# A whole-round order list, and only inverse roots left on GpSimd, in a four-layer graph network kernel

## The reference

```
attn = softmax(masked scores); o = attn @ v
x2 = layernorm(x1 + o @ Wo + bo) * g2 + be2
y  = layernorm(x2 + gelu(x2 @ W1 + b1) @ W2 + b2) * g3 + be3
x  = layernorm(x + y)
```

## Time and profile before

| | |
|---|---|
| median of three runs | 2414.89 us |
| the profiled execution | 2414.36 us |
| its span, first to last instruction | 2412.5 us |
| TensorE busy | 2108.8 us, 87% |
| VectorE busy | 1676.3 us, 69% |
| ScalarE busy | 1367.9 us, 57% |
| GpSimd busy | 380.9 us, 16% |
| mean granted TensorE clock | 0.948 of full |

### The profile page before, as it was taken

One profiled execution on the slowest core, in us unless ns is written; L12 is line 12 of the kernel. 1 busy time (PEld: TensorE's weight loads), 2 busy tenths in 40 slices (PEclk: granted clock), 3 DMA queues, 4 the chain that ended last, 5 costly groups with the idle time before them and its releaser, 6 DMA issues.

```text
span 2412.5 us, 56320 instructions
## 1 busy us (share of the span) xinstructions
PE 2108.8 (87%) x21445; PEld 1816.0 (75%) x21445; DVE 1676.3 (69%) x4767; ACT 1367.9 (57%) x3387; POOL 380.9 (16%) x400
## 2 busy tenths in 40 slices
PE   8979569898888989898989888898989898989886
PEld 5634458888787868787888778786878788888875
DVE  6779456767676766776676767676677667676844
ACT  4557335555555646565556555565656565555554
POOL 0000111112121212121121112121212112111200
PEclk9989789999999999999999999999999999999997
DMA  7867100000000000000000000000000000000000
GB/s 265 277 238 268 53 10 2 2 28 2 29 2 27 2 28 2 28 2 29 2 2 28 2 29 2 27 2 29 2 28 2 29 2 2 28 2 10 2 10 10
DMA packets 37903, 92.68 MB, mean 38 GB/s; under 512 B 2544, under 2 KB 27120, under 8 KB 33392
## 3 DMA queue, kind: packets, MB, share of 16 engines
q1 hardware_dynamic: 37616, 88.86, 10.7%
HBM read 55.29 MB, written 33.55 MB: 37 GB/s over the span
## 4 chain that ended last, share of the span: by engine, by line
PE 57%; DVE 13%; issue 12%; ACT 5%; POOL 2%; DMA 0%; DVEq 0%; POOLq 0%; ACTq 0%
PE ps L260 16%; PE ps L262 15%; PE ps L261 15%; PE ps L1063 4%; POOL rstd L1476 2%; DVE stats L1549 2%; PE ps L1132 1%; PE ps L1274 1%; DVE pool_mem L1686 1%; DVE x L1580 1%; PE ps L1045 1%; DVE pool_mem L1670 1%; DVE pool_mem L1689 1%; PE ps L1054 1%; ACT hl_b L1328 1%
## 5 line engine op out<-in xcount | busy, mean ns | idle before, releaser
L1384 ACT ACTIVATE pool_mem<-ps,lstm_b 128x128 f32<-128x128 f32 (+2 forms) x1248 | 440.1, 411 | 329.6 <-PE ps L262 322.6
L260 PE MATMUL ps<-hl_a,w_hi 128*128 128x256 f16 (+2 forms) x1984 | 478.9, 264 | 59.4 <-DVE hl_a L1697 21.6
L261 PE MATMUL ps<-hl_a,w_hi 128*128 128x256 f16 (+2 forms) x1984 | 477.5, 264 | 0.0
L262 PE MATMUL ps<-hl_a,w_lo 128*128 128x256 f16 (+2 forms) x1984 | 477.2, 263 | 0.0
L1476 POOL TENSOR_TENSOR rstd<-ve,nhalf 128x2 f32<-128x2 f32 x224 | 182.7, 816 | 1404.9 <-DVE ve L1556 1404.9
L260 PE MATMUL ps<-hl_b,w_hi 128*128 128x168 f16 (+2 forms) x1408 | 354.6, 261 | 5.3 <-DVE hl_b L1697 3.8
L261 PE MATMUL ps<-hl_b,w_hi 128*128 128x168 f16 (+2 forms) x1408 | 354.6, 260 | 0.0
L262 PE MATMUL ps<-hl_b,w_lo 128*128 128x168 f16 (+2 forms) x1408 | 354.5, 260 | 0.0
L260 PE MATMUL ps<-pool_mem,w_hi 128*128 128x128 f16 (+2 forms) x1536 | 329.8, 241 | 21.3 <-DVE pool_mem L1691 21.2
L261 PE MATMUL ps<-pool_mem,w_hi 128*128 128x128 f16 (+2 forms) x1536 | 329.5, 241 | 0.0
L262 PE MATMUL ps<-pool_mem,w_lo 128*128 128x128 f16 (+2 forms) x1536 | 329.2, 240 | 0.0
(11 more groups left out here) (234 smaller groups left out, 4859.1 us busy)
## 6 DMA issues: line engine op xcount, KB each, us to landing
xa<-in_x SPq DMA_DIRECT2D x32, 512.0 KB, 5.5
h_scratch<-pool_mem SPq DMA_DIRECT2D x16, 1024.0 KB, 4.3
pool_mem<-h_scratch SPq DMA_DIRECT2D x16, 1024.0 KB, 7.1
pool_mem<-in_wpack SPq DMA_DIRECT2D x16, 704.0 KB, 4.0
o_scratch<-act_in SPq DMA_DIRECT2D x16, 512.0 KB, 2.9
act_in<-o_scratch SPq DMA_DIRECT2D x16, 512.0 KB, 4.8
out<-xb SPq DMA_DIRECT2D x16, 512.0 KB, 3.4
row<-in_rows SPq DMA_DIRECT2D x1, 1408.0 KB, 10.8
```

Of the source, the lines that this page charges most:

```text
L260: nc.tensor.matmul(o, l[0], r[0], start=first, stop=False, skip_group_check=True)
L261: nc.tensor.matmul(o, l[0], r[1], start=False, stop=False, skip_group_check=True)
L262: return nc.tensor.matmul(o, l[1], r[0], start=False, stop=last, skip_group_check=True)
L1384: op = nc.scalar.activation(gates[s][:, g, m * w:(m + 1) * w], ps[s][:, g, m * w:(m + 1) * w], ACT.Tanh, bias=lstm_b[:, bias:bias + 1], sc ...
```

## The change

1. `x1_bias` and `x2_bias` are gone. The products of `attn_out` and `mlp_down` get one more matrix multiplication for each 128 nodes: a matrix of ones times a matrix whose rows 0 and 32 hold the high and low part of the bias (the rest is zero).
2. The multiplication of the probabilities moves from GpSimd's `probs` into VectorE's `invert_sums`.
3. `xa_bias` moves to VectorE as `shift_xa`, works in place on xa, and stands early in the tile, soon after `norm_g1`. With it xa is read until `norm_g3`, so the transfer of the next x waits for that step.
4. GpSimd keeps the roots.
5. ORDER and the rule that plays it twice give way to ROUND, a list of a whole round, in which each entry names its stream (0 or 1) and, by `:` or `+`, whether it belongs to this tile of the stream or to its next one. The two halves of the list need not be alike.
6. SyncE's loop asks for both streams' next inputs before it stores both; the signal gat_ok starts one tile ahead, so that `turn_y` can wait for the previous tile's last step.

```diff
+ROUND = """
+1:norm_g1.1 1:xa_bias.1 1:k.0 0:inp4 0:cell4 1:scores.0 1:turn_x1.1 1:exps.0 0:hid4 0:inp5 1:v.1 1:q.1 1:turn_probs.0
+1:k.1 0:cell5 0:hid5 1:attend.0 1:scores.1 1:exps.1 0:inp6 1:attn_out.0 1:norm_g2.0 1:turn_probs.1 0:cell6 0:hid6
...
+0:turn_xc.1 0:gat_mix.0 1:gcn1.1 0:gat.1 0:norm_l3.0 0+turn_y.0 1:inp0 1:cell0 0+norm_l0.0 1:hid0 1:inp1 0:gat_exps.1
...
+def rounds(n):
+    return [(name, s, n + after if after else n) for s, after, name in ROUND]
...
+                for j, name in enumerate(("bo", "b2")):
+                    nc.vector.tensor_scalar(abias[0:1, j, :], row[0:1, ROWS.index(name), :], WSCALE, None, ALU.mult)
...
                 def load_next(s, n):
...
-                        sp.wait_ge(*pre_ok.at(s, n, h, "xa"))
+                        sp.wait_ge(*ln_step.at(s, n, h, "l1.t"))
...
-                        if with_sums:
-                            mm = nc.tensor.matmul(tok(s, bank)[:, b, :], sums[:, 0:P], gbias[:, 0, :], start=False, stop=True,
+                        if with_row is not None:
+                            mm = nc.tensor.matmul(tok(s, bank)[:, b, :], with_row[0], with_row[1], start=False, stop=True,
...
-                    dense(s, h, hl_a[s], h * HTOK, "wo", BANK_B[h]).then_inc(tok_ps.of(s, h), 1)
+                    dense(s, h, hl_a[s], h * HTOK, "wo", BANK_B[h], (ones_row[:, :], abias[:, 0, :])).then_inc(tok_ps.of(s, h), 1)
...
-                def probs(s, n, h):
...
                 def invert_sums(s, n, h):
...
+                        dve.wait_ge(*smax_ok.at(s, n, h, f"inverse{b}"))
+                        nc.vector.tensor_tensor(prob[s][h][:, b, :, :], prob[s][h][:, b, :, :],
+                                                ssum[s][:, i:i + HEADS].unsqueeze(2).broadcast_to([P, HEADS, P]), ALU.mult)\
+                            .then_inc(prob_ok.of(s, h), 1)
...
                 def add_attn(s, n, h):
-                    dve.wait_ge(*pre_ok.at(s, n, h, "x1"))
...
-                                                                     xb[s][:, blocks(h), :], ALU.mult, ALU.add))
+                                                                     x1[s][:, blocks(h), :], ALU.mult, ALU.add))
...
+                def shift_xa(s, n, h):
+                    dve.wait_ge(*feat_ps.at(s, n, h, "xp"))
+                    dve.wait_ge(*x_ok.at(s, n, h, "x1"))
+                    nc.vector.tensor_tensor(xa[s][:, blocks(h), :], xa[s][:, blocks(h), :], half_row("be3"), ALU.add)\
+                        .then_inc(pre_ok.of(s, h), 1)
```

More of the change, by code:

```diff
@@ L77 @@
 PARTS = 2
[L78 to L83, removed]
@@ L84 @@
-mix1.0 gcn0.1 gcn1.0 mix1.1 gcn1.1 inp0 cell0
-""".split()
[L86 to L102, removed]
+ROUND = """
@@ new lines @@
+1:norm_g1.1 1:xa_bias.1 1:k.0 0:inp4 0:cell4 1:scores.0 1:turn_x1.1 1:exps.0 0:hid4 0:inp5 1:v.1 1:q.1 1:turn_probs.0
+1:k.1 0:cell5 0:hid5 1:attend.0 1:scores.1 1:exps.1 0:inp6 1:attn_out.0 1:norm_g2.0 1:turn_probs.1 0:cell6 0:hid6
+1:turn_x2.0 1:attend.1 0:pack4 1:attn_out.1 1:norm_g2.1 1:mlp_up.0 1:gelu_split.0 0:inp7 1:turn_x2.1 0:cell7
+1:mlp_down.0 0:hid7 1:mlp_up.1 1:norm_g3.0 1:gelu_split.1 0:inp8 0:cell8 0:hid8 1:mlp_down.1 1:norm_g3.1 0:inp9
+0:cell9 0:hid9 1:norm_l1.0 1:norm_l1.1 0:inp10 0+norm_y 0:cell10 0:hid10 1:mix0.0 1:mix0.1 0:turn_state.0 0:norm_l2.0
@@ new lines @@
+0:turn_state.1 1:gcn0.1 1:gcn0.0 0:turn_xc.0 1:mix1.1 1:mix1.0 0:gat.0 0:gat_exps.0 0:norm_l2.1 1:gcn1.0 0:turn_att.0
+0:turn_xc.1 0:gat_mix.0 1:gcn1.1 0:gat.1 0:norm_l3.0 0+turn_y.0 1:inp0 1:cell0 0+norm_l0.0 1:hid0 1:inp1 0:gat_exps.1
+1:cell1 0+cheb.0 0:turn_att.1 1:hid1 0:gat_mix.1 0+conv.0 1:inp2 1:cell2 1:hid2 1:inp3 0+norm_g1.0 0:norm_l3.1
+0+xa_bias.0 0+turn_y.1 0+norm_l0.1 0+turn_x1.0 1:cell3 1:hid3 0+cheb.1 0+v.0 1:pack3 0+q.0 0+conv.1 0+norm_g1.1 0+k.0
+1:inp4 1:cell4 0+scores.0 1:hid4 0+exps.0 0+xa_bias.1 0+turn_x1.1 1:inp5 1:cell5 0+turn_probs.0 0+v.1 0+q.1 0+k.1
@@ new lines @@
+0+attend.0 0+scores.1 1:hid5 1:inp6 0+exps.1 0+attn_out.0 0+norm_g2.0 1+norm_y 0+turn_probs.1 1:cell6 1:hid6
+0+attend.1 0+turn_x2.0 1:pack4 0+attn_out.1 1:inp7 1:cell7 1:hid7 0+norm_g2.1 1:inp8 0+mlp_up.0 0+gelu_split.0
+0+turn_x2.1 1:cell8 1:hid8 0+mlp_down.0 0+norm_g3.0 0+mlp_up.1 0+gelu_split.1 1:inp9 1:cell9 0+norm_l1.0 1:hid9
+0+mlp_down.1 0+norm_g3.1 1:inp10 1:cell10 0+norm_l1.1 1:hid10 0+mix0.0 0+mix0.1 1:turn_state.0 0+gcn0.0 1:norm_l2.0
+0+gcn0.1 0+mix1.0 0+mix1.1 1:turn_xc.0 1:turn_state.1 0+gcn1.0 1:gat.0 1:norm_l2.1 1:gat_exps.0 0+gcn1.1 1:turn_att.0
@@ new lines @@
+1:turn_xc.1 1:gat_mix.0 1:gat.1 1:norm_l3.0 1+turn_y.0 0+inp0 0+cell0 1+norm_l0.0 0+hid0 0+inp1 1:gat_exps.1 0+cell1
+1+cheb.0 1:turn_att.1 0+hid1 1:gat_mix.1 1+conv.0 1+norm_g1.0 1+xa_bias.0 0+inp2 0+cell2 0+hid2 0+inp3 1:norm_l3.1
+1+turn_y.1 1+turn_x1.0 1+norm_l0.1 0+cell3 0+hid3 1+cheb.1 1+v.0 0+pack3 1+q.0 1+conv.1
+""".split()
+ROUND = [(int(entry[0]), int(entry[1] == "+"), entry[2:]) for entry in ROUND]
+def rounds(n):
+    return [(name, s, n + after if after else n) for s, after, name in ROUND]
```

76 lines of the change are left out of this document (33 added, 43 removed).

## The result

| | before | after |
|---|---|---|
| median | 2414.39 us (4 runs) | 2275.15 us (4 runs) |
| the profiled execution, its span | 2414.36, 2412.5 us | 2281.25, 2279.1 us |
| mean granted clock | 0.948 | 0.969 |

The ratio of the times is 0.943 (95% interval 0.941 to 0.945): 139 us faster, where 47 were forecast, and outside the range of 2310 to 2440. The direction was right, the size was not. On another chip the changed kernel ran at 0.945 (0.943 to 0.946) of the kernel before.

A forecast was written before the change was run, and what follows sets the result against it. TensorE was taken to set the time. Per round, waits -6.0, bias rows +1.8 and clock -2.5 gave -6.7; over 8 rounds -54, start +7, so 2414.4 became 2367 us, with an 8-in-10 range of 2310 to 2440.

The forecast's parts named there:

- What went: TensorE waits in phase three's rounds that the new list and the moved additions would remove: 17.0 us per round.
- `turn_state`: TensorE's wait for cell 10, 2.0 us per half; both halves of mix0 ahead of it would save 1.4 us per round.
- What comes: New TensorE waits under the new list, chains less their covers: 11.0 us per round, range 5.5 to 16.5.
- `attn_out.1`: Directly behind attend.1, it would wait for ScalarE's high and VectorE's low part: 2.4 and 1.9, together 4.3 us per round.
- `turn_x1.1`: A 6.0 us chain from conv.1's addition to x1, with 5.0 us between: about 1.1 late per half, 2.2 per round.
- `turn_probs.1`: New wait behind scores.1 for masks, exponentials, reciprocals and VectorE's multiplication: 1.3 and 0.2 us, together 1.5 per round.
- the low bound: Lower end for the new waits, half the count: 5.5 us per round, which gave 2367 - 44 = 2323 us.
- the clock: TensorE's loss at granted clock 0.96, 10.3 us per round; a quarter, 2.5, taken as regained, bounds 0 and 10.3.
- Rival 3: The clock comes back whole: 10.3 instead of 2.5 us per round gained, 62 us more, 2305 us; chance 0.13.
- The bias rows: TensorE's new work, 16 products of 256 columns per round at 0.11 us: 1.8 us per round on the path.
- The start: Where one stream is alone, the chains to cheb.0 and turn_x1.0 have 4 and 3 us less beside them: +7 us.
- The direction that I weighed: VectorE's 96 moved instructions could each hold a GpSimd root by 0.4 us, 38 us at worst; nothing was taken.

The follow-up runs named there:

- list-only kernel: The kernel before with only the whole-round list and its rules, GpSimd keeping the biases and probabilities and TensorE having no bias rows: 2333.4 us, ratio 0.967.
- work-only kernel: The kernel before with its half-round list played twice, only the work moved (bias rows to TensorE, probabilities and xa + be3 to VectorE): 2367.9 us, 0.982.
- kernel with idle work: The changed kernel with GpSimd also doing additions and multiplications of the old size at the old places into a buffer nobody reads: 2335.4 us, 0.968.
- the three slides of `turn_y`: The kernel before with turn_y.0 ahead of inp1; then also norm_y earlier; then turn_y.0 ahead of inp0 and cell0, VectorE's place included: 2439.9, 2403.2, 2451.2 us.

## Why the prediction was wrong

Measured per round are here the five rounds from turn to turn of both kernels, the waits of each step summed and divided by five.

What went, forecast and measured: `cheb` 6.9 and 6.8; `turn_x2.1` with cell 8 4.3 and 4.3; `inp7` 2.7 and 2.4; `attend.1` 1.7 and 1.8; `turn_state` 1.4 and 3.7. Together 17.0 and 19.0. This side of the sum held but for `turn_state`, which was taken 2.3 too low.

**The step that failed is "What comes": 11.0 us per round forecast, 4.8 measured.** `attn_out.1` 4.3 and 3.1; `turn_x1.1` 2.2 and nothing; `turn_probs.1` 1.5 and 0.8; the graph attention 1.5 and 0.1; small ones 1.5 and 0.8 at `mix0`. I took the chains at their length in the trace of before, with GpSimd's disturbance and with what stood ahead on VectorE's queue there, and set them against the new covers. The disturbance is the smaller part of the error: in the list-only kernel, where it is still on, the same five items are 6.4 us per round, so to end it took 1.6 off. Why the other 4.6 did not come is not shown item by item. About half of the term was the low bound that I gave for it; with that alone the forecast was still 2323.

By this account waits fall by 19.0 - 4.8 = 14.2 us per round, and TensorE's idle time falls by 13.7; waits for its own instructions and gaps too short to be listed are 0.5 longer.

**The second step is the clock: 2.5 us per round taken, about 5.4 measured.** TensorE's busy time fell by 3.6 us per round with 1.8 us of bias rows added to it, and its time at half clock fell from 20.5 to 8.3 us. Rival 3 had this direction, at 0.13, and would have given all 10.3 back. The two trials with `turn_y` moved back show what I had not drawn from the earlier trace rows: in the new list a microsecond of added wait at `cheb` costs 1.3 to 1.4 more through the clock over the whole window, and 1.0 in a round from turn to turn with `turn_y` moved fully back (12.1 us longer, 6.1 of them idle and 6.0 busy). But this is no constant. In the work-only kernel `cheb` waits 7.2 us per round just so, TensorE is idle 10.2 us more than in the changed kernel, and its busy time is only 1.6 us longer; the change itself gave back 5.4 us of clock for 13.7 of idle time, 0.4. What the clock costs behind a wait depends on the list around it, and why it differs so is not shown.

**The bias rows** were taken at 1.8 us per round, 14 in all. No run here measures them alone at that price: they cost 0 to 12 of the kernel's time.

**The disturbance** was forecast as 4.3 us of waits per round and nothing else, with VectorE coming out even. Its busy sum did (182.4 against 184.4), but by the kernel with idle work it was worth 57 us, 5.4 of it in each round (249.3 against 243.9) and the rest in the start and the end. It had made waits of its own, and lengths inside chains that would have been waits under the new list (`turn_x2` 23.3 us in the list-only kernel). The parts nearly add up: 79 for the list, 57 for the disturbance, 0 to 12 back for the rows, 124 to 136 against 136 to 139; the hand-over is what may be missing.

**The round** was measured at 256.6 us, over a window that ended in the lighter last stretch; from turn to turn it is 261.1. This changed no term but the clock's base.

The start was forecast at +7. Outside the five rounds of the windows the changed kernel is 47 us shorter (1106.9 to 1059.8); three more rounds at 17.2 would be 52. The 5 us between are the start and the end together, of the size forecast.

The Trainium skill (TensorE: Matmul & The Clock Gate, The HAM clock gate) has the clock go with idleness. In the runs here it fell behind single waits of 2.5 and 3.6 us, and the earlier trace rows show it at 0.50 with TensorE busy, which is behind such a wait and no evidence against the page, as I had used it.

The Trainium skill (GPSIMD Engine Reference, Specifications) has VectorE and GpSimd contend for their shared interface. The direction that I weighed, VectorE's moved work holding up roots, is not to be seen. A root takes 837 ns at the median where it took 704, but that came with the list: it takes 836 in the list-only kernel and 697 in the work-only kernel. VectorE's waits for roots went the same way, 17 us before, 45 with the list alone, 24 with the work alone and 42 with both. The other direction, GpSimd's additions holding up VectorE, was the one worth up to 57 us. The root in the changed kernel, and in the work-only kernel:

```profile
L1494 POOL TENSOR_TENSOR rstd<-ve,nhalf x204: 691/837/1132, 458.8 to 2273.7; 128x2 f32<-128x2 f32 x102
...
L1489 POOL TENSOR_TENSOR rstd<-ve,nhalf x204: 697/697/1104, 459.0 to 2359.2; 128x2 f32<-128x2 f32 x102
```

The list of what would show it: no `cheb` wait, x at 0.48 us, nothing but roots on GpSimd, VectorE at 181, all so; waits of 19 per round were 14.5, and the round of 250 was 244.

## What to carry to other kernels

Price a wait of the engine that sets the time at its length and the clock behind it, and take the clock's part from a trial in the list at hand: here it was 1.0 to 1.4 of the wait in one list, and 0.2 to 0.4 of the idle time when other kernels are compared. Do not price a new list by chains measured under the old one without a trial of the list alone: more than half of the new waits did not come. Before a step is moved to cover a wait, read on every engine's queue what stands ahead of the instructions that feed the chain: the three slides of `turn_y` that were right on TensorE's queue failed on ScalarE's, on VectorE's and on a bank. Large two-input operations of GpSimd cost time even where nobody waits for them, when VectorE feeds the engine that sets the time: here 88 us of VectorE's and 57 of the kernel's.
